# Causal masks of the transposed scores added in PSUM by VectorE instead of by TensorE, with a new order of calls

## What is computed

```python
sim  = einsum('bhid,bhjd->bhij', q, k)            # q already scaled
sim  = where(triu(ones((n, n)), k=1), -max, sim)  # causal mask
attn = softmax(sim)
out  = attn @ v
adj  = clip(attn + eye(n), 0, 1); deg = adj.sum(-1)
feats = v
for l in range(2):                                # two hops over the graph
    h = adj @ (feats @ gnn_w[l] + gnn_b[l]) / deg
    feats = gelu(h + feats)
out = out + feats @ lin_w + lin_b
```

## Time and profile before

| | |
|---|---|
| median of 3 runs | 1490.47 us (1489.58 to 1495.8) |
| the profiled execution's own time | 1495.98 us |
| its span (first to last instruction) | 1494.2 us |
| PE busy | 1379.5 us, 92% |
| DVE busy | 1193.5 us, 80% |
| ACT busy | 996.4 us, 67% |
| POOL busy | 363.8 us, 24% |
| mean granted clock of PE | 0.974 of full speed |

### The profile page before, as it was taken

The page is one execution under the profiler, slowest core; times in us unless marked ns, Lnnn a source line. Parts: engine busy times, 40 slices in busy tenths (PEclk is TensorE's granted clock), DMA queues, the critical chain, the costliest instruction groups (busy, mean ns, idle before and its releaser), DMA issues. The chain is left out here.

```text
span 1494.2 us, 28152 instructions
## 1 busy us (share of the span) xinstructions
PE 1379.5 (92%) x9560; PEld 1067.2 (71%) x9560; DVE 1193.5 (80%) x3498; ACT 996.4 (67%) x2376; POOL 363.8 (24%) x442
## 2 busy tenths in 40 slices
PE   5899999999999999999999999998878999999895
PEld 3577887788778878778778778776556666666663
DVE  5388888888887888888888888775888888888875
ACT  3367776677667767767667766774566787778573
POOL 1023122221222112212232123212322332222211
PEclk9699999999999999999999999998799999999999
DMA  5012111211111111211112111310310010101100
GB/s 137 1 33 54 38 30 29 45 42 30 29 44 43 30 29 35 52 30 29 29 44 44 30 30 43 84 34 12 92 23 13 21 23 19 22 19 23 29 12 21
DMA packets 40664, 53.25 MB, mean 36 GB/s; under 512 B 11678, under 2 KB 23882, under 8 KB 40522
## 3 DMA queue, kind: packets, MB, share of 16 engines
q1 hardware_dynamic: 40522, 51.46, 15.0%
HBM read 9.89 MB, written 1.05 MB: 7 GB/s over the span
## 5 line engine op out<-in xcount | busy, mean ns | idle before, releaser
L1151 ACT ACTIVATE t<-PS 128x512 f32<-128x512 f32 (+3 forms) x384 | 190.5, 496 | 172.2 <-PE PS L689 116.2
L1651 DVE TENSOR_TENSOR t<-t 128x512 fp32r<-128x512 f32 (+3 forms) x384 | 210.0, 554 | 7.8 <-ACT t L1152 7.1
L1152 ACT ACTIVATE t<-PS 128x512 fp32r<-128x512 f32 (+3 forms) x384 | 190.5, 496 | 0.0
L739 PE MATMUL PS<-t 128*128 128x512 f32 (+3 forms) x384 | 144.6, 377 | 22.4 <-ACT t L1185 22.1
L1308 ACT ACTIVATE t<-PS,t 128x128 f32<-128x128 f32 x256 | 113.3, 464 | 68.0 <-DVE t L1903 68.0
L686 PE MATMUL PS<-t 128*128 128x512 f32 (+3 forms) x384 | 145.4, 379 | 4.8 <-DMA t<-t 2.2
L1484 POOL TENSOR_TENSOR t<-t 128x16 f32<-128x16 f32 x32 | 92.8, 2902 | 234.1 <-DVE t L1752 234.1
L660 PE MATMUL PS<-t 128*128 128x512 f32 (+3 forms) x384 | 141.0, 383 | 6.5 <-DVE t L1634 3.6
L1448 POOL TENSOR_TENSOR t<-t 128x256 f32<-128x256 f32 x64 | 39.4, 615 | 401.3 <-DVE t L1671 401.3
L704 PE MATMUL PS<-t 128*66 128x512 f32 (+3 forms) x384 | 135.2, 352 | 0.0
L687 PE MATMUL PS<-t 65*128 65x512 f32 (+3 forms) x384 | 134.6, 350 | 0.0
(11 more groups left out here) (206 smaller groups left out, 3687.7 us busy)
## 6 DMA issues: line engine op xcount, KB each, us to landing
t<-t SPq DMA_DIRECT2D x184, 128.0 KB, 2.3
t<-t SPq DMA_DIRECT2D x62, 256.0 KB, 3.4
t<-in_c_rot SPq DMA_DIRECT2D x4, 512.0 KB, 5.5
t<-in_L_ffn_wqkv SPq DMA_DIRECT2D x2, 768.0 KB, 6.0
t<-in_L_attn_Wv SPq DMA_DIRECT2D x2, 512.0 KB, 7.6
out<-t SPq DMA_DIRECT2D x4, 256.0 KB, 2.3
t<-in_L_ffn_w SPq DMA_DIRECT2D x2, 341.0 KB
t<-in_L_attn_x SPq DMA_DIRECT2D x2, 256.0 KB, 3.3
```

Source lines behind the costliest of these rows:

```text
L739: e.matmul(dst, F2[:, jb, :], Eh[:, o:o + n], start=(jb == 0), stop=False)
L1151: e.activation(Es[:, k % NS, 0:n], b[:, 0:n], ACT.Exp).then_inc(a_es.up((t, k)), 1)
L1152: e.activation(Eh[:, o:o + n], b[:, 0:n], ACT.Exp).then_inc(a_eh.up((t, k)), 1)
L1651: e.tensor_tensor(El[:, o:o + n], Es[:, k % NS, 0:n], f32(Eh[:, o:o + n]), ALU.subtract).then_inc(d_el.up((t, k)), 1)
```

## The change

- PE no longer issues the third matmul (L689) of the eight diagonal tiles; `cmB`, its bf16 copy of the mask, and the copy that made it are gone.
- DVE gets a new helper `acausal(t, k)`, called for tiles 0 to 3 and 8 to 11: it waits for `p_sc` of the tile, adds the float32 mask in PSUM to the first 128 columns of the tile, and raises a new signal `d_sm`. ACT's exponential of a diagonal tile waits for `d_sm` instead of `p_sc`.
- The order of the calls in the loop over heads is new on PE, ACT and DVE; on POOL one pair is swapped. What the helpers do is otherwise the same.

```diff
             def scores(t, k):                      # PE
-                m = e.matmul(b[:, 0:n], K2[...], Q2[...], start=False, stop=not diag)
-                if diag:
-                    m = e.matmul(b[:, 0:P], identB[:], cmB[:, 1, :], start=False, stop=True)
-                m.then_inc(p_sc.up((t, k)), 1)
+                e.matmul(b[:, 0:n], K2[...], Q2[...], start=False,
+                         stop=True).then_inc(p_sc.up((t, k)), 1)
...
+            def acausal(t, k):                     # DVE
+                q.wait_ge(ld["cm"], 16)
+                q.wait_ge(*p_sc[t, k])
+                s = bank(2 + k % 2)[:, 0:P]
+                e.tensor_tensor(s, s, cm[:, 1, :], ALU.add).then_inc(d_sm.up((t, k)), 1)
...
             def scores(t, k):                      # ACT
-                q.wait_ge(*p_sc[t, k])
                 q.wait_ge(*(d_el[t, k - NS] if k >= NS else d_el[t - 1, k + NTL - NS]))
                 q.wait_ge(*p_hop[t - 1, k])
+                q.wait_ge(*(d_sm if jb >= 4 * c else p_sc)[t, k])
```

More of the change, by code:

```diff
@@ L301, in program @@
         d_max = signal("d_max", maxes)
+        d_sm = signal("d_sm", [(t, k) for t, k in by_tile if tiles[k][1] >= 4 * tiles[k][0]])
         d_nm = signal("d_nm", heads)
@@ L832, in tensor @@
                 graph2(t - 1, 8)
+                smax(t + 1, 0)
+                smax(t + 1, 1)
                 scores(t, 2)
-                graph2(t - 1, 10)
-                scores(t, 3)
                 tailT(t - 2, 0)
@@ L846, in tensor @@
                     linear(1, 6)
-                tail(t - 2, 0)
+                av(t, 0)
+                scores(t, 4)
                 smax(t + 1, 3)
@@ L851, in tensor @@
                 scores(t, 5)
-                scores(t, 6)
+                tail(t - 2, 0)
                 smax(t + 1, 4)
@@ L884, in tensor @@
                     qkv(0)
-                proj(t + 2, 0, 2)
+                av(t, 9)
+                av(t, 7)
+                smax(t + 1, 11)
+                proj(t + 2, 1, 3)
                 av(t, 8)
-                proj(t + 2, 1, 3)
                 av(t, 10)
-                smax(t + 1, 11)
                 av(t, 11)
+                graph2(t, 0)
                 smax(t + 1, 10)
-                graph2(t, 0)
                 graph2(t, 2)
@@ L1269, in scalar @@
                 share(t, 0)
-                mrow(t + 1)
                 gelu2(t - 1)
@@ L1273, in scalar @@
                     square(0)
+                mrow(t + 1)
                 hopend(t, 0)
@@ L1819, in vector @@
                     rotate(0)
+                acausal(t, 0)
+                acausal(t, 1)
                 scores(t, 0)
@@ L1824, in vector @@
                     began(1)
-                scores(t, 1)
-                share(t - 1, 1)
-                scores(t, 2)
                 smax(t + 1, 0)
+                acausal(t, 2)
                 smax(t + 1, 1)
@@ L1848, in vector @@
                     onward_stats(2 * ((t - 18) % 4), (t - 18) // 4, 2)
-                scores(t, 7)
-                scores(t, 8)
-                scores(t, 9)
-                if t == 0:
-                    linear(5, 7)
+                acausal(t, 8)
+                scores(t, 5)
+                smax(t + 1, 6)
                 if 2 <= t < 6:
@@ L1857, in vector @@
                     onward_rest(2 * ((t - 18) % 4), (t - 18) // 4, 2)
+                share(t - 1, 1)
+                scores(t, 6)
+                projv(t + 1, 0)
+                scores(t, 7)
+                acausal(t, 9)
+                acausal(t, 10)
+                smax(t + 1, 7)
+                scores(t, 8)
+                smax(t + 1, 8)
+                scores(t, 9)
+                if t == 0:
+                    linear(5, 7)
                 projv(t + 1, 1)
                 scores(t, 10)
-                smax(t + 1, 7)
+                acausal(t, 11)
+                smax(t + 1, 9)
                 graph1(t, 0)
                 scores(t, 11)
-                smax(t + 1, 8)
+                lower(t + 2, 0, 2)
+                feats(t, 0)
                 graph2b(t - 1)
-                feats(t, 0)
-                smax(t + 1, 9)
-                lower(t + 2, 0, 2)
+                smax(t + 1, 11)
                 lower(t + 2, 1, 3)
-                smax(t + 1, 11)
                 smax(t + 1, 10)
```

75 lines of the change are left out of this document (35 added, 40 removed).

## The result

The changed kernel takes 1475.55 us (median of 4 runs, 1471.81 to 1479.28) where the kernel before takes 1490.03 (4 runs, 1489.38 to 1495.8): a ratio of 0.9894, with a 95% interval of 0.9854 to 0.9934. That is 14.5 us, or about 1%, faster. The profiled execution took 1472.74 us with a span of 1470.9, against 1494.2 before. Of these 23.3 us, 19.9 lie in the loop over heads (953.7 us from the first `mrow` to the last before, 933.8 after), 3.2 behind it, where no instruction was changed and where the granted clock was a little higher in this execution (0.97 for 0.95), and 0.2 ahead of it.

The account below looks back on a forecast made before the run. PE was taken to bound light passes, DVE's ring heavy ones. Eight passes of each kind, gaining 7.2 (even light), 7.2 (odd light), 9.6 (odd heavy) and losing 4.0 us (even heavy), give 20 us: 1490.5 to 1470.5, range 1456 to 1490.

Parts of the forecast that it names:

- The likeliest case: The forecast of 1470.5 us itself, own range 1462 to 1481, chance 0.48.
- Two rings, and each pass lasts as long as the longer: Loop over heads: PE decides light passes (27.5 even, 31.0 odd), DVE's ring heavy ones (28.9 even, 31.6 odd).
- What PE is rid of: 0.12 us a mask: PE, diagonal tiles: mask matmul plus late operation behind it, 8 x 0.12 = 0.97 us a pass, if PE alone decides.
- only its own columns: Rival: the late operation behind a mask stays, PE wins 0.04 to 0.06 us a mask; 1478.5 us, chance 0.05.
- What DVE is given: 0.21 us each, two of eight free: DVE: masks 0 and 1 fall into its wait for ACT; six additions lengthen its stretch by 1.26 us a pass.
- The wait of PE for `share`, covered by DVE's ring: Even heavy passes: late `share(t - 1, 1)` makes PE wait up to 1.1 us, which DVE's ring covers.
- Where the light passes' gain comes from: Light passes: PE decides and loses the masks' 0.97 us; 0.9 us gained per pass, even and odd.
- The forecast's own test: Prediction is wrong in size if PE's busy time in a light pass falls by less than 0.8 us.
- The waits that go out of DVE's stretch: DVE: new order removes waits at `share`, `tail` and two short gaps, 0.44 to 0.96 us a pass.
- PE alone decides: Rival: every pass loses what PE loses, 33 us in all; 1457 us, chance 0.15.
- DVE eats it: Rival: additions lengthen DVE's stretch and no wait goes; 1484 to 1495 us, chance 0.20 with no change at all.
- In ACT's way: Slower rival: masks delay ACT at tiles 1 to 3 at a pass's beginning, 15 us; 1506 us, chance 0.12.

Follow-up runs that it names:

- e5: Changed kernel with DVE's `share(t - 1, 1)` moved back ahead of the second layer-norm piece, masks still on DVE: 1473.99 us, ratio 0.9868 to the kernel before.
- e7: e5 with the causal masks of the transposed scores left out on both engines: 1460.46 us, ratio 0.9761 to the kernel before.
- e8: e5 with the masks back on PE: 1475.16 us, ratio 0.9873 to the kernel before.
- e1: Changed kernel with its new order of calls but the masks back on PE: 1487.55 us, ratio 0.9975 to the kernel before.
- e11: e8 with each mask matmul on PE issued twice: 1486.55 us, ratio 0.9947 to the kernel before.
- e4: Changed kernel with a second DVE addition, into a scratch tile, ahead of each of the eight masks: 1512.32 us, ratio 1.0136 to the kernel before.
- e3: Changed kernel with the causal masks of the transposed scores left out on both engines, `share` still late: 1472.94 us, ratio 0.9875 to the kernel before.
- e9: e8 in the eight even heavy passes (masks on PE), e5 in all others (masks on DVE): 1471.26 us, ratio 0.9852 to the kernel before.
- e10: e2 with DVE's `acausal(t, 11)` moved from ahead of `scores(t, 10)` to directly ahead of `scores(t, 11)`: 1579.18 us, ratio 1.0565 to the kernel before.
- e2: Kernel before with the masks moved to DVE, its old order of calls kept: 1622.07 us, ratio 1.0872 to the kernel before.

## Why the prediction was right, and where its steps were off

Forecast 1470.5 (1456 to 1490), measured 1475.6. The profiled execution lost 23.3 us of span where 20 were forecast, and the median fell 14.5: the profiled execution of before was the longest of its four, 6 us over the median, and that of after among the shorter, 3 us under it. The likeliest case came true. That the loop's 19.9 us hits the 20 so closely is in part luck: pass 0 gave 3.9 us that no term has.

*Two rings, and each pass lasts as long as the longer.* Right. The four kinds of passes came out at 27.73, 28.91, 30.71 and 31.57 for 27.5, 28.9, 31.0 and 31.6, one of them longer than before, as forecast. e5, e7 and e8 show the rule directly for even passes: the additions on DVE cost nothing in light ones and 0.93 us in heavy ones, the masks on PE 0.55 and 0.37. For odd heavy passes the length came out (31.57), but the price did not: the additions cost 0.36 us there, not 1.26, and without them PE still waits for DVE's L1614 (4.5 us in all in e7). What holds these passes at 31.14 then was not taken apart.

*What PE is rid of: 0.12 us a mask.* Somewhat high. In pass 14, e1 to after is (28.10 - 27.33) / 8 = 0.10; over all six even light passes it is 0.06 (28.19 to 27.73), since in some of them other waits take its place. The composition (own columns plus the late one behind) is as read from the earlier trace rows, by e11. The Trainium skill ("TensorE: Matmul & The Clock Gate", section "Back-to-back issue gap") gives the same formula price of 56 ns that the prediction named and, for a stream of weight loads and matmuls of 128 columns, 81 ns. The 0.10 of pass 14 lies above both, and what e11's second mask adds (0.06) agrees with the lower. The rival "only its own columns" had that share right and the late neighbour wrong.

*What DVE is given: 0.21 us each, two of eight free.* The size is right (0.20 start to start, 0.29 long). The Trainium skill ("VectorE: DVE Perf Modes", section "The TRN2 errata") gives (N + 151)/0.96 ns for an addition of N columns in float32, found exact at 512 and 2048; an estimate from it for 128 columns is 0.291 us. The duration in the trace agrees, 0.29, although here one operand and the result lie in PSUM. The price of 1.26 us an even heavy pass was more than what could be seen: 0.93 (e5 to e7). That is a lower bound, since e7's pass of 27.71 comes near PE's own 27.44. e4's passes at full clock, 1.11 to 1.18 us longer with the additions doubled, speak for nearly the full size.

*The wait of PE for `share`, covered by DVE's ring.* Right, by e5. But the text gave no price for the cover being gone. e3 and e1 show it: without the masks on DVE, the same wait makes even heavy passes 29.5 us (28.0 and 28.35 with `share` early), that is 8 x 1.2 to 1.6, or 10 to 12 us in all, with the low clock of three passes of e3 and one of e1 in it.

*Where the light passes' gain comes from.* Right in size, wrong in cause for a part. The text put all of it on the masks. Pass 14 fell from 28.38 to 28.10 by the order alone and to 27.33 by the masks: 0.28 and 0.77. Pass 15 fell from 31.91 to 30.96 and to 30.47: 0.95 and 0.49. The order made PE less busy with the same work, so that odd light passes ended below the forecast 31.0. This term was missing, and it hid that the masks' term was too large there (0.49 where 0.97 was forecast). In odd light passes masks on PE cost 0.83 us against none (e8 and e7), but DVE's additions cost 0.19 (e5), which the forecast had at nothing. The forecast's own test, PE less busy by at least 0.8 us in a light pass, held by luck: it fell by 1.04 and 1.32 us in passes 14 and 15, of which 0.27 and 0.83 are the order's.

*The waits that go out of DVE's stretch.* Right in kind. DVE's waits before, between 113 and 998 us, for ACT's copies of the values and of the projections:

```profile
DVE t L1616 <- ACT t L1122: 11.3, 20, 0.9
DVE t L1603 <- ACT t L1108: 9.3, 24, 0.4
```

After, no such waits are left, nor those of the earlier trace rows for `share` and `tail`. A new one has come, for the scores of the maxima (L1628 behind PE's L660, 15.0 us in all), which the forecast named for `smax` 10 alone.

*What the masks' move itself is worth.* With a good order for either side (e5 and e8) both take the same time, 1474.0 and 1475.2. The prediction's sum compared against the old order and couldn't see that. The move of the masks and a `share` left early are two ways to one result; only in a mixture (e9) do both count.

*The rivals.* "PE alone decides" is out: even heavy passes got longer. "DVE eats it" is out: they grew by 0.5 us and not 1.3, and light passes fell by 0.8 and 1.3, not 0.5 and 0.3. "In ACT's way" is out for the changed kernel: ACT's waits for masks lie at tile 9, and tile 2 has 3.0 us of them in all. As a mechanism the slower rival is real, but I had its place and size wrong: not tiles 1 to 3 with 15 us, but tile 11 above all, then tile 8, and 85 to 130 us in the old order (e10, e2). The forecast said the late masks fall "where ACT has idle time to spare", which is true of the new order alone.

*Open:* what the order does to PE in odd passes beyond the neighbours, what holds odd heavy passes without masks, and how much of the time behind the loop is chance. Pass 0's gain of 3.9 us was in no forecast; 3.2 of it are there in e1 already (40.28 us), so it is mostly the order's.

## What to carry to other kernels

Where two in-order engines run rings of nearly equal length, price a moved operation per stage by who decides there: the same additions were free in one kind of pass and cost 1 us in another. If taking a cost away changes little, look for the second limit just below before calling the cost small; here the masks looked worth 2.6 us until `share` was moved, and then 13.5. And an operation that a second engine makes between a producer and a consumer needs a place in three orders at once: look for one such place for each instance, the last ones above all, before trusting the saving.

## What the runs showed of the hardware that I had not expected

- The same PE instructions in another order had PE busy for 31.12 and 30.29 us (pass 15, before and e1, both at full clock): 0.8 us, or 2.7%, by the order alone. By the estimate above about 0.3 us of it is which operation stands behind which; the rest is open.
- A bf16 matmul of 128 columns makes the operation behind it late by about 0.08 us once (0.25 or 0.26 us start to start for 0.17), and a second one ahead of it doesn't add to that.
- A stretch of 2 us in which PE was busy for 0.74 us was followed by about 4 us at a granted clock of 0.54 to 0.61 (e3, 780 to 784 us), in which PE did half the operations. Such passes took 30.6 to 30.8 us; pass 22 of e3, with a wait of the same 1.5 us, kept the full clock and took 29.1.
